# Layernorm and projections of the next batch placed inside the attention loop, and row statistics moved from VectorE to ScalarE, in a fused attention and gated recurrence kernel

## What is computed

```python
def _L0_attn_ref(x, Wq, Wk, Wv, Wo, bo):
    q = (x @ Wq.T).reshape(N, S, H, hd).transpose(0, 2, 1, 3)
    k = (x @ Wk.T).reshape(N, S, H, hd).transpose(0, 2, 1, 3)
    v = (x @ Wv.T).reshape(N, S, H, hd).transpose(0, 2, 1, 3)
    att = jnp.einsum('nqhd,nkhd->nhqk', q, k)
    att = jax.nn.softmax(att / jnp.sqrt(jnp.asarray(hd, x.dtype)), axis=3)
    out = jnp.einsum('nhqk,nkhd->nqhd', att, v).reshape(N, S, D)
    return out @ Wo.T + bo
def _L0_ffn_ref(x, wf, uf, bf, wi, ui, bi, wc, uc, bc, wo, uo, bo, in_c):
    def step(c, xt):
        ft = jax.nn.sigmoid(xt @ wf.T + c @ uf.T + bf)
        it = jax.nn.sigmoid(xt @ wi.T + c @ ui.T + bi)
        gt = jnp.tanh(xt @ wc.T + c @ uc.T + bc)
        return (ft * c + it * gt, None)
    c_final, _ = lax.scan(step, c0, x)
    return jnp.tanh(jnp.einsum('tbi,oi->tbo', x, wo) + c_final @ uo.T + bo)
x = x + _layernorm(_L0_attn_ref(_layernorm(x, axis=-1), ...), axis=-1)
x = x + _layernorm(_L0_ffn_ref(_layernorm(x, axis=-1), ...), axis=-1)
```

## Time and profile before

| what | us |
|---|---|
| median of 3 runs | 3677.69 (3674.46 to 3743.73) |
| profiled execution, device time | 3673.58 |
| its span on the slowest core, core 0 | 3672.0 |
| spans of the other cores | 3641.7 to 3664.9 |

### The profile page before, as it was taken

One profiled execution on the slowest core, in us unless ns is written; L12 is line 12 of the kernel. 1 busy time (PEld: TensorE's weight loads), 2 busy tenths in 40 slices (PEclk: granted clock), 3 DMA queues, 4 the chain that ended last, 5 costly groups with the idle time before them and its releaser, 6 DMA issues.

```text
span 3672.0 us, 31761 instructions; the slowest of 8 cores (3641.7 to 3672.0 us)
## 1 busy us (share of the span) xinstructions
PE 1945.0 (53%) x9395; PEld 917.8 (25%) x9540; DVE 1103.3 (30%) x1978; ACT 476.8 (13%) x1033; POOL 333.0 (9%) x510
## 2 busy tenths in 40 slices
PE   1655455364463553644643011399999996888000
PEld 0322222132231221322311001144444442333000
DVE  0434233243342332333422056411111111222222
ACT  1020110111201101112011000111111111111000
POOL 0010201102101011021011100000000000010111
PEclk9767576575675665756756555699999998999555
DMA  6011211202111111012111753300000003111333
GB/s 115 21 44 24 59 37 41 58 21 53 53 28 49 46 40 51 28 48 56 29 48 57 125 129 112 89 1 12 12 12 12 12 12 52 29 32 32 114 126 120
DMA packets 167404, 186.97 MB, mean 51 GB/s; under 512 B 109886, under 2 KB 122174, under 8 KB 167230
## 3 DMA queue, kind: packets, MB, share of 16 engines
q0 software_dynamic: 53456, 151.38, 16.0%
q1 hardware_dynamic: 113792, 33.57, 3.8%
HBM read 151.68 MB, written 58.72 MB: 57 GB/s over the span
## 4 chain that ended last, share of the span: by engine, by line
PE 51%; DVE 16%; DMA 10%; issue 9%; ACT 6%; another core or an unknown queue 4%; DVEq 3%; POOL 1%; ACTq 0%; POOLq 0%; SPq 0%
PE ps_p L1574 11%; PE ps_a L1992 9%; PE ps_a L1998 9%; DMA xin<-x 5%; PE ps_p L1443 5%; PE ps_p L2085 3%; PE ps_p L2092 3%; PE ps_a L1679 2%; DVE otn L1727 2%; DVE kst L1637 2%; DVE qst L1637 2%; DMA vst<-v_scr 2%; PE ps_ot L1711 2%; PE ps_rl L1711 2%
## 5 line engine op out<-in xcount | busy, mean ns | idle before, releaser
L2022 DVE TENSOR_TENSOR cT<-cT,gat 128x512 f32<-128x512 f32 x64 | 44.3, 692 | 579.9 <-ACT gat L2012 579.9
L1711 PE MATMUL ps_ot<-pt_sb,vst 128*65 128x128 bf16 x256 | 64.2, 288 | 288.1 <-DMA vst<-v_scr 241.9
L1691 ACT ACTIVATE pt_sb<-ps_a 128x512 bf16<-128x512 f32 x128 | 76.1, 594 | 1019.8 <-PE ps_a L1679 1019.8
L2012 ACT ACTIVATE gat<-ps_a,biases 128x512 f32<-128x512 f32 x192 | 131.9, 687 | 584.5 <-PE ps_a L1998 584.5
L1574 PE MATMUL ps_p<-wq_sb,xlnT_t 128*128 128x512 bf16 x487 | 183.9, 558 | 43.2 <-DVE xlnT_t L1560 43.2
L1443 PE MATMUL ps_p<-wo_sb,zlT_t 128*128 128x512 bf16 x482 | 173.1, 535 | 59.4 <-DVE zlT_t L1429 59.0
L1663 POOL DMA_DIRECT2D vst<-v_scr x128 | 96.1, 753 | 835.8 <-DMA v_scr<-vtok 528.7
L1992 PE MATMUL ps_a<-xtT_sl,wq_sb 128*128 128x512 bf16 x500 | 132.6, 409 | 51.3 <-DMA xtT_sl<-xt_scr 45.1
L2085 PE MATMUL ps_p<-qst,gat 128*128 128x512 bf16 x495 | 120.1, 383 | 61.5 <-DMA gat<-xt_scr 34.3
L1998 PE MATMUL ps_a<-zb,wk_sb 128*128 128x512 bf16 x500 | 124.7, 391 | 0.6
L1679 PE MATMUL ps_a<-qst,kst 73*128 73x128 bf16 x512 | 111.6, 258 | 19.7 <-DVEq L1639 19.2
(11 more groups left out here) (166 smaller groups left out, 2686.3 us busy)
## 6 DMA issues: line engine op xcount, KB each, us to landing
xin<-x POOLq DMA_DIRECT2D x96, 512.0 KB, 4.7
xin<-xr POOLq DMA_DIRECT2D x32, 512.0 KB, 4.2
x<-x1t POOLq DMA_DIRECT2D x32, 512.0 KB, 3.0
out<-x1t POOLq DMA_DIRECT2D x32, 512.0 KB, 3.0
v_scr<-vtok SPq DMA_DIRECT2D x32, 256.0 KB, 2.0
vst<-v_scr POOLq DMA_DIRECT2D x128, 64.0 KB, 2.7
od<-orow SPq DMA_DIRECT2D x128, 64.0 KB, 1.8
zin<-od POOLq DMA_DIRECT2D x128, 64.0 KB, 3.2
```

The costliest lines, as they stand in the source:

```text
L1711: inst = t.matmul(psot[0:65, pk4 * 128:(pk4 + 1) * 128], vst[:, gbuf * 260 + pk4 * 65: gbuf * 260 + (pk4 + 1) * 65], pt_sb[:, gbuf * 512 + ...
L2012: ch_gev.inc(sc.activation(gat[:, gi * 512:(gi + 1) * 512], ps_a[:, pg * 512:(pg + 1) * 512], func, bias=biases[:, bcol + mt:bcol + mt + 1]))
```

## The change

The change has three parts.

1. P1's tile loop is cut into `emit_P1_front(n, tt)` (load to v store) and `emit_P1_qtr(n, tt)` (transposes of q and k into qst and kst). Batch 0 runs both for its four tiles as before. For every later batch the fronts of tiles 0 and 1 are placed inside the attention loop of the batch before, behind groups 5 and 11 (at 11 ahead of P2). After the loop come the q and k transposes of tiles 0 and 1, and then tiles 2 and 3 as before.
2. A load into xin, in P1 or P2, waits for the last reader of its own half (`xin_last`), not for a count relative to the latest one.
3. In the layernorm pass `ln_stats_sc` takes the place of `ln_stats`: the two long passes and all the small steps are on ACT. In the output projection `f_hstat` moves from DVE to ACT, as a Square and a Copy with sums.

The diff, cut to its core; the bodies of the two helpers are those of the old loop, instruction for instruction, but for the lines shown:

```diff
@@ emit_P2
         def f_xl(s, n=n, rt=rt, zbuf=zbuf, chx=ch_xd[zbuf],
-                 need=(ch_vfree.n - 1)):
+                 need=xin_last[zbuf]):
...
         P("vector", f_out)
         ch_x1.bump()
         ch_vfree.bump()
+        xin_last[zbuf] = ch_vfree.n
...
@@ the tile loop of P1 becomes two helpers; their bodies are the old loop body
-    _p2prev = None
+    tok_hist = {}
+    xin_last = {0: 0, 1: 0}
+    stk_vsp = {}
+    ODS_hist = {}
+
+    def emit_P1_front(n, tt):
...
+        def f_load(s, n=n, tt=tt, xi=xi, chx=chx,
+                   need=xin_last[buf]):
+            if need:
+                s.wait_ge(ch_vfree.sem, need)
...
+        P("gpsimd", f_load)
...
+        ln_stats_sc(P, ch_rst, xi, sqj[:], sl, s1, s2, mean,
+                    msq, rstd, D, wait=(chx, chx.n))
...
+        P("vector", f_apply)
...
+        xin_last[buf] = ch_vfree.n
...
+        P("tensor", f_tr)
...
+        P("vector", f_trev)
...
+                P("tensor", f_pmm)
...
+                P("vector", f_pev)
...
+        P("sync", f_vsp)
+        ch_vsp[buf].bump()
+        tok_hist[(n, tt)] = TOK_RDY
+
+    def emit_P1_qtr(n, tt):
...
+        TOK_RDY = tok_hist[(n, tt)]
...
+                P("tensor", f_qtr)
...
+                P("vector", f_qtrev)
...
+    for tt in range(NTIL):
+        emit_P1_front(0, tt)
+        emit_P1_qtr(0, tt)
+    stk_vsp[0] = (ch_stk.n, (ch_vsp[0].n, ch_vsp[1].n))
+
     for n in range(B):
-        for tt in range(NTIL):
...
+        STK_RDY, VSP_DONE = stk_vsp[n]
         for grp in range(NPK // 4):
...
-            if grp % 4 == 3 and _p2prev is not None:
-                emit_P2(_p2prev[0], grp // 4, _p2prev[1])
+            if grp == 5 and n + 1 < B:
+                emit_P1_front(n + 1, 0)
+            if grp == 11 and n + 1 < B:
+                emit_P1_front(n + 1, 1)
+            if grp % 4 == 3 and n >= 1:
+                emit_P2(n - 1, grp // 4, ODS_hist[n - 1])
...
+        if n + 1 < B:
+            emit_P1_qtr(n + 1, 0)
+            emit_P1_qtr(n + 1, 1)
+            emit_P1_front(n + 1, 2)
+            emit_P1_qtr(n + 1, 2)
+            emit_P1_front(n + 1, 3)
+            emit_P1_qtr(n + 1, 3)
+            stk_vsp[n + 1] = (ch_stk.n, (ch_vsp[0].n, ch_vsp[1].n))
 
     for rt in range(4):
-        emit_P2(_p2prev[0], rt, _p2prev[1])
+        emit_P2(B - 1, rt, ODS_hist[B - 1])
@@ layernorm pass ahead of the scan
-        def f_prew(v, chx=chx, xd=chx.n):
-            v.wait_ge(chx.sem, xd)
-        P("vector", f_prew)
-        ln_stats(P, ch_sum, ch_rst, xi, sqj[:], sl, s1, s2, mean, var, msq,
-                 rstd, epst[:], D)
+        ln_stats_sc(P, ch_rst, xi, sqj[:], sl, s1, s2, mean,
+                    msq, rstd, D, wait=(chx, chx.n))
@@ output projection
-        def f_hstat(v, rt=rt, he=ch_hev.n):
-            v.wait_ge(ch_hev.sem, he)
-            v.drain()
+        def f_hstat(sc, rt=rt, he=ch_hev.n):
+            sc.wait_ge(ch_hev.sem, he)
+            sc.drain()
             hrow = h_view(rt)
-            v.reduce_sum(hmean[:, rt:rt + 1], hrow, axis=AX)
-            ch_hst.inc(v.scalar_tensor_tensor(
-                sqj2[:], hrow, 1.0, hrow, AL.mult, AL.mult,
-                accum_out=hvar[:, rt:rt + 1]))
-        P("vector", f_hstat)
+            sc.activation(sqj[:], hrow, AF.Square,
+                          accum_out=hvar[:, rt:rt + 1])
+            sc.drain()
+            ch_hst.inc(sc.activation(sqj[:], hrow, AF.Copy,
+                                     accum_out=hmean[:, rt:rt + 1]))
+        P("scalar", f_hstat)
```

More of the change, by code:

```diff
@@ new lines, in emit_P1_qtr, with f_qtr, f_qtrev @@
+    def emit_P1_qtr(n, tt):
+        gti = n * NTIL + tt
+        buf = gti % 2
+        TOK_RDY = tok_hist[(n, tt)]
+        for src_tok, dst_st in ((qtok, qst), (ktok, kst)):
+            for hg in range(2):
+                trb = tr_slot()
+                def f_qtr(t, src_tok=src_tok, buf=buf, hg=hg, trb=trb,
+                          tok=TOK_RDY, tev=ch_trevx[trb].n):
+                    t.wait_ge(ch_pjev.sem, tok)
+                    t.wait_ge(ch_trevx[trb].sem, tev)
+                    for hh in range(8):
+                        h = hg * 8 + hh
+                        inst = t.transpose(
+                            ps_trx[trb][0:64, hh * 128:(hh + 1) * 128],
+                            src_tok[:, buf * D + h * 64: buf * D + (h + 1) * 64],
+                            ident_sb[:])
+                    ch_trx[trb].inc(inst)
+                P("tensor", f_qtr)
+                ch_trx[trb].bump()
+                def f_qtrev(v, dst_st=dst_st, tt=tt, hg=hg, trb=trb,
+                            trc=ch_trx[trb].n):
+                    v.wait_ge(ch_trx[trb].sem, trc)
+                    out_ap = dst_st[0:64, :].rearrange(
+                        "p (s h) -> p s h", h=16)[:, tt * 128:(tt + 1) * 128,
+                                                  hg * 8:(hg + 1) * 8]
+                    in_ap = ps_trx[trb][0:64, :].rearrange(
+                        "p (hh s) -> p s hh", hh=8)
+                    inst = v.tensor_copy(out_ap, in_ap)
+                    ch_trevx[trb].inc(inst)
+                    ch_stk.inc(v.drain())
+                P("vector", f_qtrev)
+                ch_trevx[trb].bump()
+                ch_stk.bump()
@@ L1785, in build_fused_program @@
             ch_ods[gbuf].bump()
[L1786 to L1790 removed]
+            if grp == 5 and n + 1 < B:
[4 more added lines that the diff above has]
+                emit_P2(n - 1, grp // 4, ODS_hist[n - 1])
+        ODS_hist[n] = (ch_ods[0].n, ch_ods[1].n)
+        g_vld_hist[n] = (ch_vld[0].n, ch_vld[1].n)
+        if n + 1 < B:
[6 more added lines that the diff above has]
+            stk_vsp[n + 1] = (ch_stk.n, (ch_vsp[0].n, ch_vsp[1].n))
     for rt in range(4):
[L1793 removed]
+        emit_P2(B - 1, rt, ODS_hist[B - 1])
     A_PJ = ch_pj.n
@@ L1825, in build_fused_program @@
     hms = sb("hms", [128, 32], F32)
-    sqj2 = otn[:].bitcast(BF16)
     ps_g = (ps_a,)
```

206 lines of the change are left out of this document (79 added, 127 removed).

## The result

| what | us |
|---|---|
| kernel before, median of 10 runs | 3678.35 |
| changed kernel, median of 10 runs | 3521.25 |
| ratio | 0.9576, 95% interval 0.9562 to 0.959 |
| predicted | 3520 (3495 to 3570) |
| profiled execution after, device time | 3529.89 |

Medians are over all timed executions, while ratios leave out those in which one die had a lower clock (of e2_ln 3589.28 and 3606.61 are left, and it has no ratio; e12_laststo's profile is of such an execution, so its core 4, of the other die, is read).

What follows compares the result with a forecast made beforehand. The prediction took attention as bound by a chain from engine to engine, no engine full. Attention 92 (313 - 221), layernorm pass 65, output projection zero: 157 us off 3673.6 gives 3516.6; with the median 4.1 higher, 3520, range 3495 to 3570.

Steps and rivals of the forecast that it cites:

- Boundary, 59.8 us predicted: Between batches, P2's end to first scores: 106.0 us falls to 59.8, tile 2's load and statistics hidden with 1.6 to spare.
- A front behind group 5, 16.5 us: In the attention loop: scores start 17.7 us later, 1.2 comes back, so each front costs 16.5.
- A front with P2 behind group 11, 14.8: In the attention loop: a front followed by P2 costs 14.8 us, as P2's matmuls run faster behind it.
- Attention, 92 us: Whole attention: boundaries save 313 us, fronts in the loop cost 221, so 92 is saved.
- Layernorm pass, 65 us: Pass ahead of the scan: a tile takes 4.75 us in place of 6.86, saving 65 over 31 periods.
- The cycle of one half of xin: Layernorm pass: load issue, landing, statistics and `f_apply` take 8.9 us for two tiles, 4.46 for one.
- The term beside it: Layernorm pass: a tile's 0.786 MB at 169 GB/s, the highest rate in a window, takes 4.65 us.
- Output projection, zero: Output projection: ACT's added 2.4 us per row tile fits its 4.11 us idle between two Tanh, costing nothing.
- the pass at its old pace: Rival, layernorm pass: landings stretch to 8.4 us and nothing is won there; 92 saved, 3586 us; chance 0.06.
- Late fronts: Rival, attention loop: each front waits up to 9.3 us for load and statistics; 27 saved, 3651 us; chance 0.05.
- Table reloads: Rival, output projection: Square and Copy need another ACT table, 2.6 us a row tile; 3520, or 3536 us; chance 0.04.

Runs made afterwards that it cites:

- e2_ln: Kernel before with only the layernorm pass's statistics moved to ACT; 3589.28 us in the profiled execution, 3606.61 in the other.
- e12_laststo: e8_stosp with the last stage's stores on SyncE's queue as well; ratio 0.881.
- e1_attn: Changed kernel with the old layernorm pass and `f_hstat` on DVE, so only the attention part of the change; 3594.77 us, ratio 0.9754.
- e4_fourloads: Changed kernel with four input buffers in place of two in the layernorm pass; 3493.14 us, ratio 0.9485.
- e3_hstat: Kernel before with only `f_hstat`, the output projection's row sums, moved to ACT; 3681.6 us, ratio 1.0009.
- e5_dveorder: Kernel before, statistics left on DVE, next tile's statistics issued ahead of a tile's copy out of PSUM; 3620.42 us, ratio 0.9837.
- e6_lateload: Changed kernel with the loads of the 14 fronts in the loop issued from SyncE's queue behind their group's store; 3619.36 us, ratio 0.9834.
- e8_stosp: Changed kernel with P2's store of its result on SyncE's queue in place of POOL's; 3390.03 us, ratio 0.9215.
- e11_front7: Changed kernel with the first front behind group 7, ahead of P2, instead of group 5; 3503.13 us, ratio 0.9523.
- e7_onefront: Changed kernel with the front behind group 11 put back between the batches; 3577.37 us, ratio 0.972.

## Why the prediction was right

It gave 157 us and the medians show 3678.35 - 3521.25 = 157.1. The agreement to a microsecond is chance; these are the steps.

- *Boundary, 59.8 us predicted:* 58.4. Copies at a spacing of 1.42 us, as read. A tile takes 23.2 us where the old rows gave 23.9. The load and the statistics of tile 2 were done 11.1 us after the P2 end, where I had 10.4, and `f_apply` came after 11.65, where I had 12.0: the slack was 0.6 and not 1.6 us. It held.
- *A front behind group 5, 16.5 us:* 18.1 - 0.7 = 17.4. Of the 1.2 that I let come back it was 0.7; the gross 18.1 was 0.4 above the 17.7. The first 16 matmuls take 6.42 us where the next 16 take 3.62.
- *A front with P2 behind group 11, 14.8:* from 1368.3, where the scores would have started, to 1391.51 are 23.2; less the 8.85 of a P2 alone (1331.94, the start of its transposes, to 1340.79) that is 14.4. The P2 matmuls took 3.45 from start to start for the 3.4.
- *What the sum didn't have:* P2 behind group 7 became dearer. Before, its 16 matmuls took 5.18 us, now they take 6.44 on core 1, and the block is 1.25 us longer; why isn't shown. The three groups behind P2 blocks, which wait for v, are 1.0 longer together. So the loop grew by 33.7 us and not by the 31.3 of the sum.
- *Attention, 92 us:* 89.6, and 87.5 by e1_attn alone. The loop took 2.4 us a batch more than predicted and the boundary 1.3 less, six times; the boundary from batch 0 to 1, counted from the last group's scores, went from 102.1 to 64.2, 1.9 more saved than predicted. 92 - 6.6 + 1.9 = 87, which is what core 1 shows (2034.3 - 1947.9 = 86.4). The mean is 3 us better, mostly because on cores 0, 2, 3, 4 and 5 one or two of the batches took 228.8 us in place of 232; in one of these, on core 4, the first front's first 16 matmuls took 4.97 us and not 6.42.
- *Layernorm pass, 65 us:* 67.9, and 68 by e2_ln. The cycle of one half of xin was the right bound. The landing grew from 3.6 to 3.9, as the 4.75 allowed for. The term beside it, 169 GB/s as the highest rate in a window, was no ceiling, as e4_fourloads shows with 205.
- *Output projection, zero:* e3_hstat says 1.0009. 2.4 us of ACT (2964.87 to 2967.24) go into the idle time.

The Trainium skill's rule that elementwise work belongs on VectorE ("ScalarE: Activation LUTs", "Rules for kernel authors") didn't decide: 68 us were gained by going the other way. It gives its factor of three for bf16; the passes here read f32, and one over 128x1024 takes 1.22 us on VectorE (L61 and L62 before) and 1.06 on ScalarE (L88 and L90). But e5_dveorder got 57 of the 68 us without leaving VectorE. What helped was that the work left the engine whose order made it wait.

Of the rivals, the pass at its old pace fell with e2_ln. Late fronts didn't happen, but e6_lateload shows that this rival was priced about right: its late fronts wait 8.5 to 9.9 us, and 7.9 each reach the end of the attention, where the prediction had up to 9.3. Table reloads didn't happen: none between Square, Copy and Tanh in 32 row tiles.

The last stage was taken as fixed. It added 14.5 us to the slowest core in the profiled execution, which is why that one, 3529.89, is 13 above the 3516.6 of the sum although the stages saved what they should. The median, 8.6 lower, hides this.

## What to carry to other kernels

Work that is moved into a loop that waits on its own chain isn't free: here it cost 33.7 of its 47.5 us, and it paid only with its load issued early enough to be hidden. It costs less where it stands ahead of matmuls that can use the granted clock that it leaves behind: 20 us came of that alone. On a queue in order, look for a transfer that waits for an engine with a load behind it that somebody needs: such stores held up 137 us in the attention and about 140 in the last stage, together more than the whole change gave, and moving them to another queue costs no instruction. Before a pass is moved to another engine, try another order on its own.

## What the runs showed of the hardware

**The last stage is longer on pairs of cores that seem to be in step.** It takes 249 to 255 us on a pair (0 and 1, 2 and 3, 4 and 5, 6 and 7) or 258 to 279 us, in the same kernel and on the same code. The loads land in 4.7 us on the one and in 5.5 on the other; in the changed kernel, core 1, then core 4:

```profile
xin<-x POOLq DMA_DIRECT2D x30, 512.0 KB, 5.5
```

```profile
xin<-x POOLq DMA_DIRECT2D x31, 512.0 KB, 4.7
```

What goes with it is the offset between the starts of the stage on the two cores, each counted from the start of its own core's span (that the two spans start together is assumed, no trace shows it). The undisturbed period of a tile is 8.05 us:

| kernel | offset and length of the last stage by pair, us |
|---|---|
| before | 8.1: 265; 11.3: 250; 4.3: 250; 11.9: 250 |
| changed | 7.2: 278; 11.3: 250; 13.2: 250; 3.5: 250 |
| e2_ln | 2.9, 4.2, 4.2, 12.1: all 250 |
| e3_hstat | 6.9: 276; 8.0: 265; 6.8: 270; 10.5: 251 |
| e8_stosp | 7.7: 266; 3.3: 252; 8.1: 268; 7.8: 268 |

Where the offset is within about two of one period, the stage is 14 to 29 us longer, with one exception (10.0 in e11_front7: 251); near two periods, at 15.2 and 16.6 in e6_lateload and e7_onefront, it is 8 us longer; at 5.9, stages of 252, 261 and 270 us all occur. This is a correlation over the eleven kernels that have the old last stage, not an experiment: no run here set the offset on purpose, and what the cores share remains open. "HBM Reference" of the Trainium skill, in its section "Specifications (TRN2)", has the HBM's bandwidth shared by the two cores of a pair, which fits. It makes the slowest core of two kernels with equal code differ by up to 29 us, so a stage that didn't change should be compared by core before a difference of totals is explained.

**A core moves more than the pass before showed.** 205 GB/s over 100 us around the pass of e4_fourloads (core 1), and 255 over e12_laststo's last stage (core 4, 3095.0 to 3220.5), with all eight cores running the same program. The highest window read before the change was 169. Neither is shown to be a limit.
